# One burst of P·V per group, and new orders of the attention work on three engines

## The chip, the core and the metric

The kernel runs on one core of a Trainium2 chip. The core has five engines that matter here: TensorE (PE, matrix multiplications, its weight loads shown apart as PEld), VectorE (DVE), ScalarE (ACT), GpSimd (POOL), and SyncE (SP), which issues nearly all transfers. Each engine works through its own list of instructions in order and waits on semaphores for the others. The metric is the time of one execution on the device, in microseconds, as the median of several runs.

## The reference

One transformer layer over 8 sequences of 512 tokens and 256 channels, in fp32, with 16 heads of 16 channels:

```python
q, k, v = x @ Wq + bq, x @ Wk + bk, x @ Wv + bv            # per head
probs = softmax(q @ k.T * 16 ** -0.5 + causal)
x = layernorm(x + (probs @ v) @ Wo + bo)
gate = silu((x @ fp8(gate_w)) * gate_scale)
up = (x @ fp8(up_w)) * up_scale
x = layernorm(x + ((gate * up) @ fp8(down_w)) * down_scale)
```

Here `fp8` rounds a weight to float8 and back. The attention and the feed-forward part each have their own residual sum and normalization.

## The kernel before

**Stages.** The program first prepares constants and the projections of the first two sequences (about 30 us), then runs the attention of all sequences, then the feed-forward part of all sequences, whose matrix products keep PE full to the end. The change lies in the attention stage and in the last steps that lead to the feed-forward part.

**Groups.** The attention stage has 32 groups w = 4n + g: n is the sequence (8 of them), g the group of four heads (0 to 3). The text calls a group by w, or by its g where all sequences behave alike. A group on PE holds:

- ten score units, `scores(w, u)`, u = 0 to 9: transposed scores (keys on the partitions) of one or two heads into one of two banks of PSUM, bank u % 2. Units 0 to 3 are the first key block of each head (all 512 queries); units 4 to 7 the second (384 columns) and fourth block (128); units 8 and 9 the third block of two heads each. ACT turns each unit into probabilities (`exps`, L461). A score unit may start only when the exp two units before it is done.
- six units of maxima for the group after the next, `scores_max(w + 2, u)`: scores the other way round, from which DVE reduces each row's maximum (`take_max`, L633). They alternate between two pairs of banks, so that unit u may start only when the reduction of unit u - 2 is done. `split_max` writes the maxima as two bf16 parts, `transpose_max` (L903) turns them into rows, ACT copies them out (`empty_mT`, L447), SP stores them to DRAM and loads them back into the first two rows of the query operand `q_st` (`store_mrow`, `load_mrow`). So the scores of group w + 1 come with the maximum already subtracted.
- the product of the probabilities with V, `attend(w, j)` for the key blocks j = 0 to 3, in four column strips of 32, one for each of the four heads, with a column of ones that gives the sum. Before the change it comes in two bursts: `attend_first(w)` (block 0, L997) near the end of group w, and `attend_rest(w)` (blocks 1 to 3) after unit 3 of group w + 1. ACT empties the result (`empty_y`, L466), PE transposes it (`transpose_y`, L919), DVE divides by the sums (`normalize_y`, L647 and L650), and PE transposes pairs of groups into `ynT` (`transpose_yn`, L930).
- four quarters of `work(n, g, i, half)`, i and half being 0 or 1: for g = 0 and 2 the projections q and k of the next sequence (`project_qk`, L878), for g = 1 the output projection of the last sequence (`project_o`, L947), for g = 3 the projection v of the next (`project_v`, L886). They share one bank, MB, so that the third quarter may start only when DVE or ACT and DVE have emptied the first half (`take_bank`).

**Parts of q and k.** ACT, DVE and POOL split each q and k into three bf16 parts: `hi_part` (ACT, L437), `rest_part` (DVE, L586), `mid_part` (ACT, L441), `lo_part` (POOL, L380). SP stores the parts (`store_parts`) and loads them back in the layout of the operands (`load_stack`: L248, L249, and the zero rows, L251). The first unit of maxima of group w + 2, which runs in group w, is the first reader of stack w + 2.

**Order of SP.** SP's list for one sequence is fixed: stack 3; store and load the maxima of group 1; store the parts 0 and 1 of the next sequence; maxima of group 2; stacks 0 and 1 of the next sequence; maxima of group 3; parts 2 and 3; the next x transposed; maxima of group 0 of the next sequence; its stack 2; its residual x; and, in the first three sequences, one raw feed-forward weight (`load_raw`).

**Other work of the attention stage.** DVE rounds the raw weights in 96 steps (`quantize`, L600 to L614, three steps per group from w = 5 on, the rest in w = 30 and 31), and sums up the residual (`empty_o`), its statistics (`take_stats`) and moments (`take_moments`, L676 to L680). POOL zeroes the masked triangle of the probabilities (`mask_units`, L385) and adds the output bias (`add_bias`, L376) in g = 3. In the last sequence the normalized x of the first two sequences is transposed (`first_hT`, L1015, `h_hi` on ACT, `h_lo` on DVE, L693).

## Time and profile before

| | us |
|---|---|
| median of 3 runs (554.30 to 556.21) | 554.45 |
| profiled execution, its own time | 557.38 |
| its span, first to last instruction | 555.7 |
| PE busy in the span | 527.9 (95%) |
| DVE busy | 459.4 (83%) |
| ACT busy | 316.1 (57%) |
| POOL busy | 227.3 (41%) |
| mean granted clock of PE, of full speed | 0.986 |

Times in the rows below are microseconds from the start of the span. The starts of successive rows of a timeline give what a piece really took from the engine; the duration of a matmul in the trace includes its way through the array, so that successive ones overlap. In brackets stands the idle time before the row and what ended it. The profiled execution lies 2.9 us above the median of the runs.

### The profile page before, as it was taken

To read this page: it belongs to the slowest core of one execution; us is meant where nothing else is said; L and a number is where in the kernel's file an instruction comes from. 1 tells how busy PE (TensorE), PEld (TensorE's weight loads), DVE (VectorE), ACT (ScalarE), POOL (GpSimd) and SP (SyncE) were. 2 spreads that over 40 slices of the span, in tenths; PEclk is the share of its full clock that TensorE was granted. 3 is DMA by queue.
4 is the path that set the end of the run, shared out by engine and by line. 5 is a ranking of instruction groups with operands and counts; after the bars stand their busy time and mean duration, and the time that the engine had idled before them with its cause. 6 is when DMAs were issued, how large, how long until landed. Compare 5 with 4: busy or idle time off the path is not lost.

```text
span 555.7 us, 10699 instructions
## 1 busy us (share of the span) xinstructions
PE 527.9 (95%) x3915; PEld 355.3 (64%) x3917; DVE 459.4 (83%) x808; ACT 316.1 (57%) x579; POOL 227.3 (41%) x251
## 2 busy tenths in 40 slices
PE   8979989999999999999999999998799999999992
PEld 3644546566565655666566565563478888888892
DVE  7876768898898888889888888998748888988876
ACT  3136676667676676766766657667354454436540
POOL 5003343263254334335325434423334654456542
PEclk9988999999999999999999999999899999999998
DMA  5864876657648547456554754700000101111012
GB/s 182 268 149 145 205 231 199 142 186 220 171 156 211 178 144 203 132 164 184 161 148 158 206 155 136 156 4 2 1 0 1 40 0 39 39 38 35 5 38 76
DMA packets 61548, 68.19 MB, mean 123 GB/s; under 512 B 6328, under 2 KB 55864, under 8 KB 61496
## 3 DMA queue, kind: packets, MB, share of 16 engines
q1 hardware_dynamic: 60664, 66.59, 41.9%
q10 hardware_dynamic: 832, 0.92, 0.5%
q8 instruction: 31, 0.51, 0.4%
q14 instruction: 21, 0.17, 0.1%
HBM read 37.62 MB, written 29.61 MB: 121 GB/s over the span
## 4 chain that ended last, share of the span: by engine, by line
PE 78%; DMA 7%; DVE 6%; issue 4%; SPq 2%; ACT 2%; POOL 1%; POOLq 0%; DVEq 0%; ACTq 0%
PE ps L1036 16%; PE ps L989 11%; PE ps L997 10%; PE ps L878 9%; PE ps L1156 7%; PE ps L970 6%; PE ps L947 5%; PE ps L971 4%; PE ps L886 4%; DMA m_scratch<-mrow 2%; PE ps L919 2%; DMA k_scratch<-part 2%; DMA q_st<-zero_rows 2%; PE ps L930 1%; DVE nmax L633 1%
## 5 line engine op out<-in xcount | busy, mean ns | idle before, releaser
L633 DVE TENSOR_REDUCE nmax<-ps 128x2 f32<-128x1024 f32 (+1 forms) x192 | 196.6, 1040 | 49.9 <-PE ps L971 49.3
L461 ACT ACTIVATE probs<-ps 128x512 f32<-128x512 f32 x320 | 184.1, 597 | 76.8 <-PE ps L989 75.3
L385 POOL TENSOR_SCALAR_AFFINE_SELECT probs<-probs 128x512 f32<-128x512 f32 x128 | 87.1, 694 | 209.1 <-ACT probs L461 209.1
L989 PE MATMUL ps<-q_st,k_st 98*128 98x384 bf16 (+3 forms) x512 | 122.7, 303 | 4.4 <-ACT probs L461 3.7
L412 POOL TENSOR_TENSOR f_l<-f_full,f_h 128x512 fp32r<-128x512 f32 x48 | 63.7, 1328 | 72.2 <-ACT f_h L544 72.1
L970 PE MATMUL ps<-k_st,q_st 98*128 98x256 bf16 (+2 forms) x384 | 82.3, 275 | 5.7 <-DMA k_st<-k_scratch 3.2
L971 PE MATMUL ps<-k_st,q_st 124*128 124x128 bf16 x512 | 84.3, 221 | 0.0
L997 PE MATMUL ps<-probs,v_st 128*32 128x512 f32 (+3 forms) x1024 | 82.5, 438 | 0.0
L989 PEld LDWEIGHTS ps<-q_st,k_st 98*128 98x128 bf16 x512 | 44.2, 99 | 48.9 <-issue 26.8
L539 ACT ACTIVATE sgate<-ps,s_gate 128x512 f32<-128x512 f32 x48 | 32.8, 686 | 60.5 <-PE ps L1036 60.5
L971 PEld LDWEIGHTS ps<-k_st,q_st 124*128 124x128 bf16 x512 | 46.0, 98 | 18.2 <-DVE nmax L633 13.7
L970 PEld LDWEIGHTS ps<-k_st,q_st 98*128 98x128 bf16 x384 | 37.6, 98 | 26.6 <-issue 7.8
L778 DVE SCALAR_TENSOR_TENSOR f_full<-ps,s_up,sgate 128x512 f32<-128x512 f32 x48 | 35.5, 744 | 19.5 <-ACT sgate L539 19.5
L1156 PE MATMUL ps<-w_down,f_h 128*128 128x256 f32 x192 | 45.9, 281 | 0.2 <-POOL f_l L412 0.2
L1156 PE MATMUL ps<-w_down,f_l 128*128 128x256 f32 x192 | 45.8, 281 | 0.0
L380 POOL TENSOR_TENSOR part<-rest,part 128x512 bf16<-128x512 f32 x28 | 32.4, 1158 | 32.6 <-ACT part L441 32.6
L997 PEld LDWEIGHTS ps<-probs,v_st 128*32 128x32 f32 x1024 | 28.6, 109 | 20.6 <-issue 12.7
L1036 PE MATMUL ps<-hT_h,w_gate 128*128 128x512 f32 x96 | 39.7, 414 | 0.0
L1036 PE MATMUL ps<-hT_l,w_gate 128*128 128x512 f32 x96 | 38.3, 399 | 0.0
L1036 PE MATMUL ps<-hT_h,w_up 128*128 128x512 f32 x96 | 38.2, 398 | 0.0
L1036 PE MATMUL ps<-hT_l,w_up 128*128 128x512 f32 x96 | 38.0, 395 | 0.0
L1156 PEld LDWEIGHTS ps<-w_down,f_h 128*128 128x128 f32 x192 | 36.2, 189 | 0.7 <-POOL f_l L412 0.4
(96 smaller groups left out, 823.8 us busy)
## 6 DMA issues: line engine op xcount, KB each, us to landing
q_st<-q_scratch SPq DMA_DIRECT2D x31, 384.0 KB
k_st<-k_scratch SPq DMA_DIRECT2D x31, 384.0 KB
q_scratch<-part SPq DMA_DIRECT2D x16, 384.0 KB, 2.6
k_scratch<-part SPq DMA_DIRECT2D x16, 384.0 KB, 2.8
xT<-in_attn_xT SPq DMA_DIRECT2D x8, 512.0 KB, 3.7
q_scratch<-part SPq DMA_DIRECT2D x16, 256.0 KB, 2.9
resid<-in_attn_x SPq DMA_DIRECT2D x8, 512.0 KB, 5.9
k_scratch<-part SPq DMA_DIRECT2D x15, 256.0 KB, 2.1
```

The lines of the kernel that those rows point to most:

```text
L385: pool.affine_select(out=blocks, in_=blocks, compare_op=ALU.is_ge, fill=0.0, base=0, pattern=[*pattern, [1, P]], channel_multiplier=-1).th ...
L412: pool.tensor_tensor(f_l[:, par, ic, :], f_full[:, ic % 3, :], f_h[:, par, ic, :].bitcast(F32), ALU.subtract).then_inc(flo_ready, 1)
L461: act.activation(probs[:, u, :], ps[:, u % 2, :], ACT.Exp, scale=SCALE).then_inc(exp_done, 1)
L633: dve.tensor_reduce(nmax[:, i, heads[0]:heads[-1] + 1], src, AX.X, ALU.max, negate=True).then_inc(max_taken, 1)
L778: dve.scalar_tensor_tensor(f_full[:, ic % 3, :], ps[:, UP[ic % 3], :], s_up[:, ic:ic + 1], sgate[:, ic % 3, :], ALU.mult, ALU.mult).then_i ...
L878: m = pe.matmul(ps[:, bank, :], wt[:, c, P * t:P * t + P], xT[:, n % 2, c, :], start=c == 0, stop=c == KC - 1)
L970: pe.matmul(ps[:, bank, c0:c0 + P * i], q_st[0:RP, g, h, q], k_st[0:RP, g, h, 0:P * i], start=True, stop=True)
L971: m = pe.matmul(ps[:, bank, c0 + P * i:c0 + P * i + P], q_st[0:RA, g, h, q], k_st[0:RA, g, h, q], start=True, stop=True)
L989: m = pe.matmul(ps[:, u % 2, c0:c0 + T - P * j], k_st[0:RP, g, h, P * j:P * j + P], q_st[0:RP, g, h, P * j:T], start=True, stop=True)
L997: m = pe.matmul(ps[HW * h:HW * h + HW, YB, P * j:T], v_st[:, (w // G) % 2, j, HG * g + h, :], probs[:, u, c0:c0 + T - P * j], start=j == 0 ...
L1036: m = pe.matmul(ps[:, bank, :], wt[:, c, P * ic:P * ic + P], hT[:, par, c, :], start=c == 0 and hT is hT_h, stop=c == KC - 1 and hT is hT_l)
L1156: m = pe.matmul(o, f[:, par, ic, P * tb:P * tb + P], w_down[:, ic, :], start=ic == 0 and f is f_h, stop=ic == IC - 1 and f is f_l)
```

## The change

- P·V: `attend_first` and `attend_rest` become `attend_all(w - 1)`, one burst after unit 3 of group w. The probabilities of the units 0 to 3 get a second buffer (`probs_a`, chosen by w % 2), so that the next group's exps can start before the burst; the other six units stay single (`probs_b`). `pv_done` counts once per group.
- `w_raw` has two buffers instead of three. The third raw weight is loaded into the first one, in sequence 4 instead of sequence 2, after the first weight's rounding.
- PE: the unit 0 of the maxima moves ahead of the score unit 2; unit 1 stays behind the burst but ahead of score unit 4; unit 2 comes before the score unit 6, with `transpose_y`; unit 3 before 7, unit 4 after 8, unit 5 after 9, and `transpose_yn` after it. The third quarter of `work` moves from before score unit 6 to after it; the fourth stays between 7 and 8.
- DVE: `take_stats` and `take_moments` move ahead, to before the reduction of unit 1, `normalize_y` moves behind the reduction of unit 3, and one `h_lo` moves back.
- ACT: the first `hi_part` of a group moves from after exp 2 to after exp 3 and `empty_mT`; one `h_hi` moves ahead by one exp.

The core of the diff (the renaming of `probs` in the places where it is only read by its unit is left out):

```diff
-        w_raw = [sb(f"w_raw{m}", [P, KC * I]) for m in range(3)]
+        w_raw = [sb(f"w_raw{m}", [P, KC * I]) for m in range(2)]
-        probs = carve(NU * T).rearrange("p (u t) -> p u t", u=NU)
+        probs_a = carve(2 * HG * T).rearrange("p (z u t) -> p z u t", z=2, u=HG)
+        probs_b = carve((NU - HG) * T).rearrange("p (u t) -> p u t", u=NU - HG)
+        def prob_unit(w, u):
+            return probs_a[:, w % 2, u] if u < HG else probs_b[:, u - HG]
...
@@ SP
+                if m == 2:
+                    sp.wait_ge(quant, 8 * NQ // 3)
-                sp.dma_start(w_raw[m][:].rearrange("p (k n) -> p k n", k=q),
+                sp.dma_start(w_raw[m % 2][:].rearrange("p (k n) -> p k n", k=q),
-                if n < 3:
-                    load_raw(n)
+                if n in (0, 1, 4):
+                    load_raw(min(n, 2))
@@ ACT
                 if u == 0:
-                    wait(act, pv_done, 2 * (w - 1) + 1)
+                    wait(act, pv_done, w - 1)
                 if u == HG:
-                    wait(act, pv_done, 2 * (w - 1) + 2)
+                    wait(act, pv_done, w)
                     exps(w, 2)
-                    if split:
-                        hi_part(n + 1, g)
...
                     if w + 1 < W:
                         empty_mT(w + 1)
+                    if split:
+                        hi_part(n + 1, g)
                     if w:
                         empty_y(w - 1)
                     exps(w, 4)
+                    if last_n and g > 1:
+                        h_hi(g - 2, g - 2, 1, MB)
                     if split:
                         mid_part(n + 1, g)
                     exps(w, 5)
-                    if last_n and g > 1:
-                        h_hi(g - 2, g - 2, 1, MB)
@@ DVE
                         rest_part(n + 1, g)
+                    if g > 1 and n:
+                        take_stats(n - 1, 2 * g - 4)
+                        take_stats(n - 1, 2 * g - 3)
...
                         h_lo(g - 2, g - 2, 0, MB)
-                    if g > 1 and n:
-                        take_stats(n - 1, 2 * g - 4)
-                        take_stats(n - 1, 2 * g - 3)
+                    if g == 3 and n:
+                        take_moments(n - 1)
                     if more:
                         take_max(w + 2, 1)
                         take_max(w + 2, 2)
-                    if last_n and g > 1:
-                        h_lo(g - 2, g - 2, 1, MB)
-                    if w:
-                        normalize_y(w - 1)
                     if w > G:
                         quantize(first_step(w) + 1)
                     if more:
                         take_max(w + 2, 3)
-                    if g == 3 and n:
-                        take_moments(n - 1)
+                    if w:
+                        normalize_y(w - 1)
                     if split:
                         rest_part(n + 1, g + 1)
+                    if last_n and g > 1:
+                        h_lo(g - 2, g - 2, 1, MB)
@@ PE
-            def attend_first(w):
-                pe.wait_ge(masked, 4 * w + 1)
+            def attend_all(w):
+                pe.wait_ge(masked, 4 * w + 4)
                 wait(pe, yn_ready, w)
                 pe.wait_ge(v_out, 2 * (w // G) + 2)
-                attend(w, 0).then_inc(pv_done, 1)
-            def attend_rest(w):
-                pe.wait_ge(masked, 4 * w + 4)
-                attend(w, 1)
-                attend(w, 2)
-                attend(w, 3).then_inc(pv_done, 1)
+                for j in range(TB - 1):
+                    attend(w, j)
+                attend(w, TB - 1).then_inc(pv_done, 1)
...
-                    scores(w, 2)
                     if more:
                         scores_max(w + 2, 0)
+                    scores(w, 2)
                     scores(w, 3)
                     if w + 1 < W:
                         transpose_max(w + 1)
                     if w:
-                        attend_rest(w - 1)
-                    scores(w, 4)
+                        attend_all(w - 1)
                     if more:
                         scores_max(w + 2, 1)
+                    scores(w, 4)
                     scores(w, 5)
-                    work(n, g, 1, 0)
-                    scores(w, 6)
                     if more:
                         scores_max(w + 2, 2)
                     if w:
                         transpose_y(w - 1)
+                    scores(w, 6)
+                    work(n, g, 1, 0)
+                    if more:
+                        scores_max(w + 2, 3)
                     scores(w, 7)
+                    work(n, g, 1, 1)
+                    scores(w, 8)
                     if w + 1 == W:
...
                         gate_up(0, 0, 0)
-                    work(n, g, 1, 1)
-                    scores(w, 8)
                     if more:
-                        scores_max(w + 2, 3)
+                        scores_max(w + 2, 4)
                     scores(w, 9)
                     if more:
-                        scores_max(w + 2, 4)
-                    attend_first(w)
+                        scores_max(w + 2, 5)
+                    if w + 1 == W:
+                        gate_up(0, 0, 1)
                     if g == 0 and n:
                         transpose_yn(n - 1, 1, w)
                     if g == 3:
                         transpose_yn(n, 0, w if n + 1 < B else None)
-                    if w + 1 == W:
-                        gate_up(0, 0, 1)
-                    if more:
-                        scores_max(w + 2, 5)
-            attend_rest(W - 1)
+            attend_all(W - 1)
```

## Rows read from the trace of the kernel before

**Rows 1.** Busy time by stretch: us, busy of PE, PEld, DVE, ACT, POOL, clock, DMA.

```profile
240.31:251.50 11.19, 11.19 (x92) 6.05 (x90) 10.07 (x18) 8.06 (x16) 3.97 (x5) 1.00 0.46 138
251.50:263.18 11.68, 11.68 (x104) 8.04 (x102) 10.49 (x24) 6.91 (x14) 7.00 (x8) 1.00 0.65 189
263.18:274.76 11.58, 11.58 (x96) 6.51 (x94) 9.89 (x18) 8.32 (x17) 4.53 (x6) 1.00 0.64 178
274.76:285.96 11.20, 11.20 (x100) 7.55 (x98) 9.74 (x16) 7.34 (x14) 3.77 (x5) 1.00 0.53 153
```

**Rows 2.** Timeline of PE around the two bursts of P·V (both lie between rows).

```profile
238.93 0.22 PE L971 MATMUL ps<-k_st,q_st 124*128 124x128 bf16 x1
...
240.08 0.40 PE L971 MATMUL ps<-k_st,q_st 124*128 124x128 bf16 x4
...
240.53 1.02 PE L878 MATMUL ps<-xT,w_q 128*128 128x512 f32 x2
241.39 0.38 PE L989 MATMUL ps<-q_st,k_st 98*128 98x512 bf16 x1
...
243.13 0.38 PE L989 MATMUL ps<-q_st,k_st 98*128 98x512 bf16 x1
...
244.90 0.39 PE L989 MATMUL ps<-q_st,k_st 98*128 98x384 bf16 x2
```

**Rows 3.** Timeline of PE: third quarter of work in g = 2, then in g = 0.

```profile
245.47 0.38 PE L989 MATMUL ps<-q_st,k_st 98*128 98x384 bf16 x2
...
246.70 0.38 PE L989 MATMUL ps<-q_st,k_st 98*128 98x384 bf16 x2
...
268.34 0.38 PE L989 MATMUL ps<-q_st,k_st 98*128 98x384 bf16 x2
...
269.47 0.39 PE L989 MATMUL ps<-q_st,k_st 98*128 98x384 bf16 x2
```

**Rows 4.** Timelines of PE and ACT: last quarter's hi_part, and a wait for an exp.

```profile
248.03 1.07 PE L878 MATMUL ps<-xT,w_k 128*128 128x512 f32 x2
...
249.20 0.69 ACT L437 ACTIVATE part<-ps,b_k 128x512 bf16<-128x512 f32 x1 [0.38 <-PE ps L878]
...
69.70 1.68 ACT L461 ACTIVATE probs<-ps 128x512 f32<-128x512 f32 x3
...
70.35 0.39 PE L989 MATMUL ps<-q_st,k_st 98*128 98x512 bf16 x1 [0.47 <-ACT probs L461]
```

**Rows 5.** Timelines of ACT, SP, PE and PEld: maxima out, a stack's last issue, its reader.

```profile
255.25 0.25 ACT L447 ACTIVATE mrow<-ps 32x128 bf16<-32x128 bf16 x1
...
242.69 0.32 PE L970 MATMUL ps<-k_st,q_st 98*128 98x384 bf16 x1
...
146.12 0.65 SPq L251 DMA_DIRECT2D q_st<-zero_rows  x1
...
150.91 0.10 PEld L970 LDWEIGHTS ps<-k_st,q_st 98*128 98x128 bf16 x1 [0.57 <-DMA q_st<-zero_rows]
```

**Rows 6.** Chain of waits, 100 to 345 us: total us, times, longest.

```profile
PEld ps L970 <- DMA q_st<-zero_rows: 1.9, 4, 0.7
```

**Rows 7.** Timelines of DVE and POOL: g = 3, and the bias of the last sequence.

```profile
254.53 1.23 DVE L633 TENSOR_REDUCE nmax<-ps 128x2 f32<-128x1024 f32 x1 [0.61 <-PE ps L971]
...
257.45 0.93 DVE L633 TENSOR_REDUCE nmax<-ps 128x2 f32<-128x768 f32 x1
...
261.92 0.37 DVE L676 BATCH_NORM_AGGREGATE moments<-stats 128x2 f32<-128x6 f32 x4
...
256.02 2.46 POOL L376 TENSOR_TENSOR resid<-resid,b_o 128x1024 f32<-128x1024 f32 x1
...
388.30 2.44 POOL L376 TENSOR_TENSOR resid<-resid,b_o 128x1024 f32<-128x1024 f32 x1
...
388.57 2.38 DVE L610 TENSOR_SCALAR q_d<-q_d 128x384 f32<-128x384 f32 x1
```

**Rows 8.** Timeline of PE in the last group.

```profile
392.20 0.66 PE L1015 MATMUL ps<-ident,resid 128*128 128x128 f32 x4 [3.70 <-DVE hT_l L693]
```

More of the change, by code:

```diff
@@ L210, in attention_over @@
         def attention_over(eng):
-            for s, count in [(st_full, NU * W), (max_full, NM * W), (pv_done, 2 * W), (mT_full, W),
+            for s, count in [(st_full, NU * W), (max_full, NM * W), (pv_done, W), (mT_full, W),
                              (late_in, 16 * NLATE), (scales_in, 16 * NSCALE)]:
@@ L764, in _ @@
                         take_max(w + 2, 4)
+                    if more:
                         take_max(w + 2, 5)
+                    if more:
                         split_max(w + 2)
```

33 lines of the change are left out of this document (17 added, 16 removed).

## The prediction

> **What bounds the kernel now.** I read the busy time by stretch first, then the timeline of PE over four groups, then those of DVE, ACT and SP beside it. In the attention's steady state a sequence is four groups of 11.19, 11.68, 11.58 and 11.20 us (g = 2, 3, 0, 1), together 45.65, and PE is busy in all of it, at full clock, DVE in 9.7 to 10.5 of each [rows 1]. So PE's stream sets the pace there, and only what shortens it or makes it wait counts. From w = 5 to w = 27 this pattern runs 23 groups. Before it (w = 0 to 4) PE waits for stacks and maxima from DRAM, after it (w = 28 to 31) for DVE. The feed-forward part is untouched.
>
> Inside the stream there are costs that no idle time shows. An fp32 matmul of 512 columns takes 0.86 us (240.53 to 241.39), a bf16 one of 128 columns 0.06 and one of 512 0.22 [rows 2].
>
> **One burst instead of two.** The first burst lies between the matmuls that start at 238.93 and 240.08: 1.15, less 0.06 of the first one, is 1.09 us for what streams in 0.86. The other, with `transpose_max` in front, lies between 243.13 and 244.90: 1.77 less 0.22 is 1.55, for 384 + 256 + 128 = 768 columns, 1.28 at that rate [rows 2]. Each burst so costs about 0.25 beyond its columns. One burst has 0.86 + 1.28 + 0.27 = 2.41 instead of 2.64: 0.23 less per group, 23 x 0.23 = 5.3 us. If the surplus belonged to the key blocks and not to the burst, it would be nothing.
>
> The Trainium skill says that a change of tiling mode drains TensorE (TensorEngine Tiling (Array Packing), Key Properties). It names no price; that the surplus stands at both bursts agrees with it.
>
> **The third quarter of work.** In g = 2 it takes, with the score unit before it, 245.47 to 246.70 = 1.23 us; in g = 0, where its bank has long been free, 268.34 to 269.47 = 1.13 [rows 3]. The 0.10 is the wait for DVE, which empties the bank just then; g = 1 and 3 have it too. The change puts the quarter 1.9 us later in the group (burst of block 0, maxima unit 2, `transpose_y` and score unit 6 now precede it), and DVE does nothing later there: 17 groups x 0.09 = 1.5 us gained. `transpose_yn` no longer follows a burst directly, which gives about 0.05 in 11 groups, 0.5.
>
> **The end of a group.** After the fourth quarter PE now has only score unit 8 (0.22), maxima unit 4 (8 matmuls of 128 columns, 0.46), score unit 9 (0.22) and maxima unit 5 (4 of them, 0.23) before the next group, together 1.13. ACT's order there is as before: `hi_part`, exp 8, exp 9. `hi_part` starts 1.17 after the start of the fourth quarter (248.03 to 249.20) and takes up to 0.69, an exp frees its bank 0.65 after its start (69.70 to 70.35) [rows 4]. So unit 0 of the next group can start 1.17 + 0.6 + 0.65 = 2.42 after the quarter's start, where PE would be there after 0.91 (the 0.86 and the entry after a short matmul) + 1.13 = 2.04. In g = 0 and 3 `transpose_yn` covers it (0.49 before, the difference of g = 3 to g = 2 in [rows 1]). In g = 2 it doesn't: 0.38 us in 6 groups, 2.3 lost. Before, maxima unit 3 and the burst lay there as well and covered it.
>
> **The moments.** In g = 3 `take_moments` moves ahead to before the reduction of unit 1. DVE comes to it about here: the reduction of unit 0 started 3.03 us into the group (254.53 less 251.50), now 0.22 earlier, 2.81, and from it to the end of the statistics it takes 257.45 - 254.53 = 2.92; so at 5.7, and with the 0.37 of the four aggregations the copy of the means comes at about 6.1. `add_bias` started 4.5 into the group (256.02) and follows exp 3, which comes about 0.25 later (below): 4.8, and 2.46 long, to 7.2 [rows 1, 7]. The one case in the trace of a DVE instruction of the tensor_scalar or copy kind under that addition is at 388.57: it took 2.38 us, to 390.95, the addition ran 388.30 to 390.74 [rows 7]. If the copy of the means is held likewise, to 7.3, the reduction of unit 1 starts 1.1 later, and that of unit 3 ends at 10.6, just where PE wants it for unit 5; `normalize_y` and `empty_v` then end at 11.9, and the first quarter of the next group wants the bank at 11.6. That costs 0.3 to 0.5 a sequence; 6 x 0.4 = 2.4 lost. Below: nothing, if so small a copy slips through; above: 1.1 x 6 = 6.6, if nothing is absorbed. I take 2.4, since the row shows the hold but the reductions have slack.
>
> The Trainium skill says that VectorE's modes with two ports and its instructions with two SBUF inputs contend with GpSimd for the SBUF interface (GPSIMD Engine Reference, Specifications). The row at 388.57 agrees; by the rule alone the copy waits, so the term stays.
>
> **Transfers.** Four weight loads between 100 and 345 us waited for a stack's last transfer, 1.9 us in total, 0.7 the longest [rows 6]. They read the stacks 8, 12, 14 and 18, which so had no slack. For stack 12 the last issue is at 146.12, the reader at 150.91, 4.79 later [rows 5]. The chain to a stack goes over the maxima in the same queue of SP: `empty_mT`, store, load, stack. The reader comes now 2.16 into its group instead of 2.38 (240.31 to 242.69), as the maxima precede the score unit 2, and the group before it is shorter by 0.33 to 0.37. And `empty_mT`, 3.75 into g = 3 before (251.50 to 255.25) [rows 1, 5], stands behind exps 2 and 3, and score unit 2 starts 0.44 later than before, so that the two exps ((1.68 - 0.60) / 2 = 0.54 apart [rows 4]) follow at 3.0 and 3.5 and `empty_mT` at about 4.0. Together each stack is wanted about 0.8 earlier against its issue. For the stacks without slack that is up to 0.8 of waiting each, less the 0.4 of the moments in g = 3 for stacks 14 and 18. The third of the four (stack 14) has the third raw weight behind it; with that weight's load the delay moves to stack 22. I take 4 places x 0.5 = 2.0 lost, less 0.3 that the first pass loses at the old place: 1.7. Ends: 0 (the stores land when the traffic ahead of them is through, however late they are issued), and 4.7 (all six stacks after g = 1 and g = 3 that lie within 1 us).
>
> **Start and end.** In w = 0 there is no burst any more (-1.1), but `hi_part` comes after exp 3, behind a stack that lands late, and the exp wait above applies in w = 0 and 2; where a stack is waited for, score unit 2 now lies behind it (+0.22) and the maxima's copy comes later (+0.3), twice. Together +0.4, between -1 and +1.5. At the end PE waits 3.70 us for `h_lo` on DVE [rows 8]; statistics of two blocks (0.66) now stand before that `h_lo`, and the last burst, 0.86 longer, follows the last work: of both I count 1.2, as one score unit, `transpose_y` and one burst's surplus leave that stretch. Between 0 and 2.5.
>
> **Sum.** -5.3 - 1.5 - 0.5 + 2.3 + 2.4 + 1.7 + 0.4 + 1.2 = +0.7 us. Against the profiled execution, 557.38 us, that is 558.1; the median of the runs is 554.45, so 555.1. POOL's own orders are unchanged, its mask of units 8 and 9 ends some 1.3 us into the next group by the exps' times above and is wanted after score unit 3, at 3.1; the second buffer of `probs_a` takes away a wait for the burst that nothing else now has. SP's new wait for `quant` in sequence 4 is met by then (32 steps are done in w = 15).
>
> **Rivals.**
>
> 1. *The hidden costs don't come* (faster). The moments' copy isn't held and the stacks land in time: -4.1 more, so 551.0; if the exp wait is covered too, 548.7. For it: DVE's 128 x 4 copy is tiny, and the store of the maxima is only 8 KB behind bigger transfers. Against: rows 6 and 7. It decides from a stack delay under 0.2 us and a hold under 0.3.
> 2. *The stacks become the bound* (slower). The time from `empty_mT` to the stack's last byte doesn't shrink with the group. If it grows by 0.5 (the parts of g + 1 are now stored later and lie before the maxima's store), the wait applies to 13 stacks at about 0.5, another +5: 560. For it: the four waits already there. Against: from w = 18 on no weight load shows one. It decides from 0.8 us later than now.
> 3. *The burst's surplus stays* (slower). It belongs to the blocks: +5.3, 560.4. Against: the second burst has three blocks and about the surplus of the one.
> 4. *DVE becomes the bound in g = 0 and 2*: `rest_part` comes after the last quarter, so `split_max` ends 14.1 into the group, where PE wants it at 14.3. If late by 0.3 in 12 groups: +2.2 after what the exp wait absorbs, 557.3.
>
> **Chances.** Forecast 0.40 (with its own range 552.0 to 557.2); rival 1 0.33; rival 2 0.13; rival 3 0.05; rival 4 0.09, of which half reads as no change. Likeliest is 555.1. The range reaches from rival 1 to rival 2: 549.5 to 560. About 0.5%, 2.8 us, is what a measurement of this kernel can tell from no change. Faster 0.34, same 0.42, slower 0.24.
>
> **What would show it.** P·V: x1024 as before, but one burst per group, 2.4 us between its neighbours. `issue` and ACT: weight loads of unit 0 wait for exp 8 by 0.3 to 0.4 in g = 3. DVE: L680 in g = 3 takes over 1 us. PEld waits for the zero rows more than 4 times, over 2 us. The third quarter's 0.10 is gone in g = 1, 2, 3. The period of four groups is 44.8 to 45.3 instead of 45.65. The prediction is wrong if the period comes below 44.7 (rival 1) or if g = 2 and 0 become longer than 11.6 without `transpose_yn` (rivals 2 and 4).

## The result, and the profile after

The kernel after takes 562.98 us (560.56 to 563.85, four runs) against 554.56 of before beside it: 1.0138 times, 95% interval 1.0102 to 1.0175. Ratios here and below are worked out from the single runs and not from the two medians, and leave out runs over 1.5% above the fastest of their kernel (three of `mom_late`, one of `moments_back`, one of before). The kernel after is slower by 1.4%; 555.1 was predicted, and the range ended at 560. The profiled execution took 562.99 us, its span 561.3, 5.6 more than before. Counted by the starts of the groups' first score units, 0.95 us of the 5.6 arise before w = 5, 2.3 in the 23 groups from w = 5 to 27, where a gain of 0.9 was expected, and 2.4 after.

Busy time by stretch of the kernel after, of w = 17 to 20 (g = 1, 2, 3, 0; the last three are the first three groups of [rows 1]):

```profile
231.25:242.32 11.07, 11.07 (x99) 7.64 (x98) 9.73 (x17) 7.08 (x15) 3.79 (x5) 1.00 0.49 146
242.32:253.63 11.31, 11.02 (x93) 6.17 (x90) 9.91 (x17) 8.03 (x16) 3.83 (x5) 1.00 0.50 143
253.63:265.11 11.48, 11.48 (x102) 8.01 (x102) 10.93 (x24) 7.14 (x14) 5.96 (x6) 1.00 0.64 185
265.11:277.66 12.55, 11.74 (x95) 6.39 (x93) 10.33 (x16) 8.20 (x17) 4.75 (x6) 1.00 0.72 186
```

Against [rows 1], g = 1 is shorter by 0.13 and g = 3 by 0.20; g = 2 is longer by 0.12 and g = 0 by 0.97. The four take 46.4 together instead of 45.65, where 44.8 to 45.3 was forecast. The last column but two is the granted clock: it is full in both.

Timeline of PE, in w = 21 (a burst), in w = 22 (the end of g = 2) and in w = 16:

```profile
280.97 1.08 PE L1008 MATMUL ps<-probs_a,v_st 128*32 128x512 f32 x8
281.86 1.49 PE L1008 MATMUL ps<-probs_b,v_st 128*32 128x384 f32 x24
283.28 0.28 PE L981 MATMUL ps<-k_st,q_st 98*128 98x256 bf16 x1
...
299.14 0.38 PE L1000 MATMUL ps<-q_st,k_st 98*128 98x256 bf16 x2
299.36 0.39 PE L982 MATMUL ps<-k_st,q_st 124*128 124x128 bf16 x4
300.04 0.38 PE L1000 MATMUL ps<-q_st,k_st 98*128 98x512 bf16 x1 [0.29 <-ACT probs_b L469]
...
222.09 0.34 PE L981 MATMUL ps<-k_st,q_st 98*128 98x384 bf16 x1 [1.10 <-DMA q_st<-zero_rows]
```

The whole burst takes 283.28 - 280.97 = 2.31. Before, the second burst took 1.45 and the first 1.00, with 0.10 lost in front of it ([rows 2]: 1.15 less 0.06); 2.55 has become 2.31, so the saving of 0.24 per group is real. But four maxima matmuls that stream in 0.23 (299.36) are followed by a score unit only 0.68 later: 0.45 of waiting for exp 8, at the end of each g = 2. And in w = 16 the first maxima unit waits for a stack.

The chain of waits from 100 to 345 us:

```profile
PEld ps L981 <- DMA q_st<-zero_rows: 6.8, 6, 1.9
PE ps L981 <- DMA q_st<-zero_rows: 2.2, 3, 1.1
PE ps L1000 <- ACT probs_b L469: 1.7, 6, 0.3
```

The stacks' row is 6.8 us in six waits, where it was 1.9 in four [rows 6]. All the long ones stand in g = 0, for the stack of g = 2. Timeline of SP before the row at 222.09:

```profile
208.80 0.33 SPq L244 DMA_DIRECT2D k_scratch<-part  x1
209.24 0.38 SPq L270 DMA_DIRECT2D xT<-in_attn_xT  x1
211.05 0.33 SPq L260 DMA_DIRECT2D m_scratch<-mrow  x1
214.25 0.64 SPq L264 DMA_DIRECT2D q_st<-m_scratch  x1
215.00 0.34 SPq L253 DMA_DIRECT2D q_st<-q_scratch  x1
```

The 8 KB of maxima are stored at 211.05, and SP waits 3.2 us for them, until 214.25, before it loads them and then the stack. 512 KB of x transposed were issued 1.8 us ahead of them. That neighbour isn't new. In the kernel before, the same group has:

```profile
207.85 0.38 SPq L265 DMA_DIRECT2D xT<-in_attn_xT  x1
209.66 0.33 SPq L255 DMA_DIRECT2D m_scratch<-mrow  x1
212.19 0.64 SPq L259 DMA_DIRECT2D q_st<-m_scratch  x1
```

There too the load is issued 1.8 us ahead, and the store takes 2.5 us. Last, the moments, on DVE and POOL in g = 3:

```profile
306.35 1.21 DVE L687 TENSOR_SCALAR veps<-moments 128x4 f32<-128x4 f32 x1
307.47 0.16 DVE L688 COPY means<-moments 128x4 f32<-128x4 f32 x1
307.54 2.07 DVE L641 TENSOR_REDUCE nmax<-ps 128x2 f32<-128x768 f32 x2
```

POOL's bias addition ran from 305.17 to 307.53, and `veps` ended with it.

### The profile page after: what moved, and what is told of

The parts are those of the page before. It is cut to its first block, busy times and chain, and to the rows that moved or that the text cites. A ratio compares the mean times of both kernels' runs of the same rounds, so it can differ in the third digit from the quotient of the medians.

```text
span 561.3 us, 10698 instructions
## 1 busy us (share of the span) xinstructions
PE 525.5 (94%) x3915; PEld 356.8 (64%) x3917; DVE 462.9 (82%) x808; ACT 314.4 (56%) x579; POOL 222.1 (40%) x251
## 4 chain that ended last, share of the span: by engine, by line
PE 67%; DMA 10%; DVE 8%; ACT 4%; issue 4%; SPq 3%; POOL 1%; POOLq 0%; DVEq 0%; ACTq 0%
PE ps L1043 15%; PE ps L1008 10%; PE ps L1000 8%; PE ps L1161 7%; PE ps L889 7%; PE ps L981 6%; DMA q_st<-zero_rows 6%; PE ps L958 5%; DVE nmax L641 3%; PE ps L982 3%; PE ps L897 2%; DMA m_scratch<-mrow 2%; PE ps L930 2%; DMA k_scratch<-part 2%; PE ps L1022 1%
## 5 line engine op out<-in xcount | busy, mean ns | idle before, releaser
L641 DVE TENSOR_REDUCE nmax<-ps 128x2 f32<-128x1024 f32 (+1 forms) x192 | 194.2, 1040 | 36.9 <-PE ps L982 35.4
L469 ACT ACTIVATE probs_b<-ps 128x512 f32<-128x512 f32 x192 | 109.0, 596 | 37.5 <-PE ps L1000 35.5
L1000 PE MATMUL ps<-q_st,k_st 98*128 98x384 bf16 (+3 forms) x512 | 113.6, 303 | 6.9 <-ACT probs_b L469 5.3
L393 POOL TENSOR_SCALAR_AFFINE_SELECT probs_b<-probs_b 128x512 f32<-128x512 f32 x96 | 61.1, 654 | 105.1 <-ACT probs_b L469 105.1
L469 ACT ACTIVATE probs_a<-ps 128x512 f32<-128x512 f32 x128 | 71.8, 597 | 50.7 <-PE ps L1000 50.6
L981 PEld LDWEIGHTS ps<-k_st,q_st 98*128 98x128 bf16 x384 | 37.7, 98 | 44.8 <-issue 18.8
L393 POOL TENSOR_SCALAR_AFFINE_SELECT probs_a<-probs_a 128x512 f32<-128x512 f32 x32 | 22.2, 694 | 110.4 <-ACT probs_a L469 110.4
L1008 PEld LDWEIGHTS ps<-probs_b,v_st 128*32 128x32 f32 x768 | 28.4, 114 | 37.0 <-issue 32.7
L1008 PE MATMUL ps<-probs_b,v_st 128*32 128x384 f32 (+2 forms) x768 | 50.2, 394 | 0.0
L474 ACT ACTIVATE yT<-ps 128x512 f32<-128x512 f32 x32 | 19.1, 597 | 40.5 <-PE ps L1008 40.5
```

Source lines behind the costliest of these rows:

```text
L393: pool.affine_select(out=blocks, in_=blocks, compare_op=ALU.is_ge, fill=0.0, base=0, pattern=[*pattern, [1, P]], channel_multiplier=-1).th ...
L469: act.activation(prob_unit(w, u), ps[:, u % 2, :], ACT.Exp, scale=SCALE).then_inc(exp_done, 1)
L641: dve.tensor_reduce(nmax[:, i, heads[0]:heads[-1] + 1], src, AX.X, ALU.max, negate=True).then_inc(max_taken, 1)
L981: pe.matmul(ps[:, bank, c0:c0 + P * i], q_st[0:RP, g, h, q], k_st[0:RP, g, h, 0:P * i], start=True, stop=True)
L1000: m = pe.matmul(ps[:, u % 2, c0:c0 + T - P * j], k_st[0:RP, g, h, P * j:P * j + P], q_st[0:RP, g, h, P * j:T], start=True, stop=True)
L1008: m = pe.matmul(ps[HW * h:HW * h + HW, YB, P * j:T], v_st[:, (w // G) % 2, j, HG * g + h, :], prob_unit(w, u)[:, c0:c0 + T - P * j], start ...
```

## The experiments

Ratios are to the kernel before in the same series, with their 95% intervals; before had medians of 556.2 to 557.0 us in these series. A "piece" is the time from the start of one unit's matmuls to the start of the next.

### First series: one part alone, or one part back

`burst_alone` is the kernel after with the lists of PE, DVE and ACT in the order of before: one burst after score unit 3 and nothing else moved. `pe_order_back` has only PE's list in the old order. `moments_back` has only this undone on DVE:

```diff
-                    if g == 3 and n:
-                        take_moments(n - 1)
                     if more:
                         take_max(w + 2, 1)
...
                     if more:
                         take_max(w + 2, 3)
+                    if g == 3 and n:
+                        take_moments(n - 1)
```

`raw_alone` is the kernel before with two raw buffers and the third load in sequence 4.

> The changed kernel with the orders of PE, DVE and ACT put back to those of before: what is left of the change is the single burst, the second buffer of the units 0 to 3 and the raw weight's later load. Theory A (the burst gains, the new orders lose): about 0.23 us per group in 23 steady groups, 1.1 more in w = 0, so 548 to 550 us, ratio to before 0.988 to 0.992; the steady period of four groups is 44.7 to 44.9 instead of 45.65. Rival B (the burst itself loses, because the stacks become the bound at any shorter period): ratio at or over 1.0, with waits for the zero rows over 1 us in g = 0.

> The changed kernel with PE's order of units put back to that of before (one burst, after score unit 3); DVE and ACT keep the new orders. Theory A (PE's new order causes the stack waits, by a later score unit 9, a later empty_mT and an earlier reader): the waits for the zero rows fall back to 0.7 us or less each, ratio to before 0.99 to 1.00. Rival (the orders of DVE and ACT cause them, by the parts stored later): ratio stays over 1.01.

> The changed kernel with take_moments alone put back behind the reduction of unit 3 in g = 3. The changed kernel's veps instruction takes 1.2 us there under POOL's addition of the bias. If that hold costs what the prediction said, 0.3 to 0.5 us a sequence: about 2.4 us faster than the changed kernel, 560.5, ratio to before 1.010. Rival (the hold is absorbed, since PE waits for the stack in the next group anyway): the same time as the changed kernel within 0.5 us, ratio 1.014.

> The kernel before with two raw weight buffers and the third weight's load moved from sequence 2 to sequence 4, nothing else. Theory A: within 0.1% of before (0.3 us gained at stack 14 and in w = 12, as much lost at stack 22). Rival: the load in sequence 4 makes stack 22 late by over 1 us, ratio 1.002 to 1.004.

| | us | ratio |
|---|---|---|
| burst_alone | 571.91 | 1.0261 (1.0232 to 1.0290) |
| pe_order_back | 584.31 | 1.0491 (1.0457 to 1.0524) |
| moments_back | 563.04 | 1.0081 (1.0051 to 1.0111) |
| raw_alone | 555.99 | 0.9978 (0.9957 to 0.9998) |

The raw weights are not the cause: `raw_alone` is 0.2% faster than before, if anything. The single burst in the old orders loses 2.6%, nearly twice as much as the whole change. So the theory that the burst gains and the new orders lose fell: the new orders repair about half of what the burst breaks. They do so only together. `pe_order_back` keeps the new orders of DVE and ACT under the old one of PE, and loses 4.9%, where no loss was expected. In its profile no weight load waits for the zero rows from 100 to 345 us, as expected, but PE now waits for DVE instead: 3.3 us in five waits for `rest_part` (`rest`), 5.4 in five for `normalize_y` (`yn`), and 3.0 in five for the residual sum (`resid`). Windows of `burst_alone`, g = 2, 3, 0, then the end of g = 2 on PE:

```profile
243.17:254.80 11.63, 11.26 (x92) 6.14 (x90) 10.16 (x18) 7.82 (x15) 3.69 (x6) 1.00 0.48 138
254.80:267.15 12.35, 11.80 (x105) 8.15 (x102) 10.74 (x24) 7.00 (x14) 7.16 (x8) 1.00 0.65 183
267.15:279.56 12.41, 11.77 (x96) 6.61 (x94) 9.88 (x17) 8.31 (x17) 4.93 (x6) 1.00 0.81 223
```

```profile
253.98 0.22 PE L979 MATMUL ps<-k_st,q_st 124*128 124x128 bf16 x1
254.57 0.40 PE L979 MATMUL ps<-k_st,q_st 124*128 124x128 bf16 x4 [0.37 <-DVE nmax L641]
254.80 0.38 PE L997 MATMUL ps<-q_st,k_st 98*128 98x512 bf16 x1
255.22 0.92 PE L894 MATMUL ps<-w_v,xT 128*128 128x256 f32 x3
```

Where the first burst used to stand, between maxima units 4 and 5, PE now waits 0.5 us (254.57 less 253.98 less 0.06) for the reduction of unit 3. The next group's first quarter comes another 0.2 late (255.22 less 254.80 less 0.22) and takes 0.1 longer. That is more than the 0.24 saved. This gave the new theory: the first burst was cover for DVE and ACT at the end of a group.

The hold of the moments was left undecided: the time fell by some 0.6% against the 1.0138 of another series, but in the profiles the 23 groups take 265.1 against 265.5 us, since stacks that land late take back most of it.

### Second series: what is PE's work worth?

`cut_before` and `cut_after` leave out 384 of the 512 queries of key block 0 of P·V:

```diff
-                    m = pe.matmul(ps[HW * h:HW * h + HW, YB, P * j:T], v_st[...],
-                                  probs[:, u, c0:c0 + T - P * j], start=j == 0, stop=j == TB - 1)
+                    m = pe.matmul(ps[HW * h:HW * h + HW, YB, P * j:T if j else P], v_st[...],
+                                  probs[:, u, c0:c0 + (T - P * j if j else P)], start=j < 2, stop=j == TB - 1 or j == 0)
```

`pad_burst` adds to `burst_alone`, between maxima units 4 and 5, the four matmuls of block 0 once more, for nothing. `two_bursts` is the kernel after with the first burst back between score unit 9 and maxima unit 5.

> The kernel before with key block 0 of P.V multiplied for its first 128 queries alone (it leaves out the other 384 columns of that block in every group), so that the first burst of a group, near its end, streams 128 columns instead of 512: 0.65 us less of PE's work per group, with nothing moved. Theory P (the prediction's: PE's stream sets the pace in the steady state, so what shortens it counts in full): 0.65 x 31 = 20 us less, 537. Theory C (the first burst covers work of DVE and ACT at a group's end: reductions whose banks the next maxima and the transposition want, exps 8 and 9; without it PE waits there): at most a third of it comes, 549 to 555, and the chain of waits shows PE waiting for the reductions of nmax.

> The kernel after with the same cut (the single burst streams 1280 - 384 = 896 columns; it leaves out 384 columns of block 0). Theory P: 20 us less than after, 543. Theory C with the stacks: the burst lies in the middle of the group, where DVE and ACT have slack, but the stacks from DRAM and exp 8 bound g = 0 and 2, so the groups shrink by the cut in g = 1 and 3 alone: 8 to 14 us less, 549 to 555, with more waiting for the zero rows.

> The single burst with all orders of before (571.9), and with a pad at the place of the old first burst: the same four matmuls of block 0 into the bank of y, whose result the real burst overwrites. It is PE work for nothing, 1.1 us in each of 32 groups. Theory P: 35 us more, 607. Theory C: the pad lies in waits that are there already (the weight loads of the transposition and of the next scores waited for nmax): 572 to 580, and these waits vanish from the chain.

> The kernel after, but with P.V in two bursts again: block 0 between score unit 9 and maxima unit 5 of its own group, blocks 1 to 3 at the place of the single burst; the double first key blocks, the raw weights and all other orders are those of after. Theory P: the surplus of 0.23 us comes back in about 27 groups: 6 us more than after, 569. Theory C: the first burst covers again exp 8 in g = 2 and 1, and the end of the reductions: these waits go (0.3 in 12 groups), the stack is wanted later by as much as the burst lies behind its issue; 559 to 563, same as after or below. If it falls under 556, the single burst itself is what costs, also on the new orders.

| | us | ratio |
|---|---|---|
| cut_before | 552.29 | 0.9915 (0.9888 to 0.9942) |
| cut_after | 547.78 | 0.9855 (0.9806 to 0.9903) |
| pad_burst | 577.84 | 1.0387 (1.0347 to 1.0427) |
| two_bursts | 564.13 | 1.0137 (1.0104 to 1.0170) |

In `cut_before` the first burst's piece falls from 1.00 to 0.44 us. Its windows, g = 1, 2, 3, 0:

```profile
226.71:237.35 10.64, 10.63 (x101) 7.55 (x98) 9.30 (x15) 7.33 (x14) 3.64 (x6) 1.00 0.50 153
237.35:248.23 10.88, 10.87 (x93) 6.02 (x90) 10.07 (x18) 7.90 (x15) 3.68 (x6) 1.00 0.52 148
248.23:259.80 11.57, 11.37 (x105) 8.02 (x102) 10.63 (x24) 7.01 (x14) 7.14 (x8) 1.00 0.60 180
259.80:271.35 11.55, 11.27 (x96) 6.48 (x94) 9.88 (x17) 8.30 (x17) 4.93 (x6) 1.00 0.74 190
```

Against [rows 1] that is 0.56 less in g = 1, 0.31 in g = 2, 0.11 in g = 3 and next to nothing in g = 0. In all 31 groups 17 us of PE's work went and the time fell by 4.7 (0.85% of 556; the interval is 3.2 to 6.2). In the kernel after, the same cut (0.64 a group in the single burst, 20 us) brings 2.8%, 15.7 us, more than was expected by the theory of cover and less than by that of PE's pace. Its place is another, the middle of the group, but so is the kernel, and the 1.0138 comes from another series. `pad_burst` is the mirror: 32 x 1.1 = 35 us of useless work on `burst_alone` cost 1.26%, 7 us. So PE was busy throughout in the kernel before, but other engines were almost as late as PE at the end of the group.

`two_bursts` has after's time. In its g = 3 (12.97 us) PE waits 0.75 for the reduction of maxima unit 1, which stands behind the held moments, and 0.64 for the first burst, whose bank `normalize_y` empties late in the new DVE list. It doesn't tell the burst's worth.

### Third series: after's waits, one by one

`xt_after` moves one load of SP, `xt_before` does the same to before:

```diff
                 load_mrow(n, 3)
+                if n + 2 < B:
+                    load_xT(n + 2)
                 if nxt:
                     store_parts(n + 1, 2)
                     store_parts(n + 1, 3)
-                if n + 2 < B:
-                    load_xT(n + 2)
```

`hi_after` puts the second `hi_part` behind exp 8. `mended` has this, the early load, `moments_back`, and the third quantize step ahead of `rest_part`.

> The kernel after, where SP issues the load of the next x transposed (512 KB) behind the load of the maxima of group 3, ahead of the stores of the parts 2 and 3, instead of behind them and so ahead of the maxima of the next group 0. Theory S (in after, the stores of these maxima wait behind the 512 KB, and with them the stack of g = 2, whose landing PE waits for in g = 0 and in the start): the store takes 2.4 us instead of 3.2 to 3.7, stacks 4, 6, 18, 22, 26 and 30 land about 1 us earlier, the zero rows' 9.0 us of waits fall under 3, g = 0 takes 11.7 every time; 4 us less than after, 558 to 560. Rival: the stack is limited by its own 768 KB and the load of x that goes with it; then nothing changes, 562 to 564.

> The kernel after, where the second hi_part of a group comes behind exp 8 on ScalarE, not ahead of it. Theory E (the next group's first score unit waits for exp 8, which stands behind hi_part, 0.45 us in g = 2 and about 0.2 with the entry of the matmul behind it): g = 2 takes 10.8 instead of 11.30, g = 3 0.1 less, 3 to 4 us less than after over 6 passes if the stacks don't take it back, 559. If the stacks set the pace of a pass, all of it is given back in g = 0: 562 to 563, with g = 2 short and g = 0 longer than 12.4.

> The kernel after with four things mended at once: x transposed loaded earlier (as in the run before the last), hi_part behind exp 8, the moments behind the reduction of maxima unit 3, and VectorE's third quantize step of a group ahead of rest_part (which waits for hi_part there, 9.5 us in all), no longer behind it. PE's stream without waits would be 10.9, 10.8, 11.2 and 11.3 us in g = 1, 2, 3 and 0, 44.2 against 45.65 of before. Theory C with S and E: the waits were all that stood against the burst's gain; the pass takes 44.3 to 45.0, 551 to 555. If the first half of the old burst is needed as cover whatever is mended, the pass stays at 46 and the time at 560.

> The kernel before with x transposed loaded earlier alone, as a control. Before waits 1.9 us for the zero rows of four stacks in the steady state, and more in its start: theory S expects 1 to 3 us less than before, 553; the rival, no change.

| | us | ratio |
|---|---|---|
| xt_after | 559.02 | 1.0039 (1.0016 to 1.0061) |
| hi_after | 568.63 | 1.0208 (1.0172 to 1.0244) |
| mended | 570.00 | 1.0233 (1.0201 to 1.0265) |
| xt_before | 554.35 | 0.9953 (0.9934 to 0.9971) |

The stacks' theory held: 1.0138 has become 1.0039. Timeline of SP in `xt_after`, in the same group as above:

```profile
209.59 0.33 SPq L260 DMA_DIRECT2D m_scratch<-mrow  x1
210.97 0.64 SPq L264 DMA_DIRECT2D q_st<-m_scratch  x1
```

The maxima's store takes 1.4 us instead of 3.2, and the waits for zero rows fall from 6.8 us in six to 2.4 in five. The store isn't short every time: in w = 23 it takes 3.1 us even so (3.7 in after), and in w = 28 PE waits 3.1 us for a stack (1.9 in after). The load also helps the kernel before.

`hi_after` removed its wait and lost more, beyond both times that were expected. The end of its g = 2:

```profile
257.79 0.39 PE L982 MATMUL ps<-k_st,q_st 124*128 124x128 bf16 x4
258.04 0.38 PE L1000 MATMUL ps<-q_st,k_st 98*128 98x512 bf16 x1
259.38 0.92 PE L897 MATMUL ps<-w_v,xT 128*128 128x256 f32 x3 [0.97 <-DVE rest L594]
```

Score unit 0 no longer waits (0.25 after unit 5 of the maxima), but the first quarter starts 1.34 after it instead of 0.22, since `rest_part`, behind the later `hi_part`, empties its bank. The fourth quarter, `hi_part`, `rest_part` and exps 8 and 9 are one chain; whoever goes first, PE has too little behind the fourth quarter to cover it. `mended` has the same wait (1.34 in w = 19) and missed both of its expected times; its further parts can't be read apart.

### Fourth and fifth series: cover, moments, and the burst again

`ty_late` is `xt_after` with `transpose_y` behind the fourth quarter in g = 2, and the third quantize step ahead of `normalize_y` there:

```diff
+                    late = n + 1 < B and g == 2
-                    if w:
+                    if w and not late:
                         transpose_y(w - 1)
                     scores(w, 6)
...
                     work(n, g, 1, 1)
+                    if late:
+                        transpose_y(w - 1)
                     scores(w, 8)
```

`mom_late` is `xt_after` with `take_moments` behind `empty_v(n + 1, 1)`. `both_late` has both, and in the last sequence maxima unit 0 behind score units 2 and 3. `xt_raw_before` is before with the early load and the two raw buffers. `both_two_bursts` is `both_late` with the first burst back between score unit 9 and maxima unit 5. `ends_back` is `both_late` with maxima unit 0 behind units 2 and 3 in the first sequence too, and the last sequence's `h_lo` at their old places on DVE.

> The kernel after with x transposed loaded earlier (xt_after, 559.0 us), and in g = 2 the transposition of y behind the fourth quarter of work instead of ahead of score unit 6, with VectorE's third quantize step ahead of normalize_y there. That puts 0.44 us of PE between the fourth quarter and the end of the group, without holding anything else of the group's end. Theory E (the fourth quarter, hi_part, exp 8 and rest_part are a chain that needs about 0.45 us more cover than after's order leaves in g = 2): g = 2 takes 10.85 instead of 11.30, g = 3 0.17 less at its start; 3 to 4 us less than xt_after, 555.5. Rival: the chain moves to the bank of the next group's first quarter, as when hi_part was put behind exp 8; 559 or more.

> xt_after, and take_moments behind the emptying of the second half of v, where POOL's bias addition has ended. Theory M (VectorE, held about 1.0 us by that addition, has no idle time in g = 3 and comes late to the second half of v, whose bank the next group's first quarter wants: 0.32 us of waiting and 0.1 of entry at the start of g = 0, 0.07 in the third quarter): g = 3 and g = 0 lose these 0.5 together, 5 passes, 2.5 us less than xt_after, 556.5. Rival: the hold is absorbed; 559.

> Both of these, and in the last sequence maxima unit 0 behind the score units 2 and 3 (its stack lands 3 us late there and nothing lies behind it). If E and M hold and add up: 559.0 - 3.5 - 2.5 - 0.5 = 552.5, better than before (556.9 in that series) and than before with the earlier load (554.4). Rival: the shorter groups wait for the stacks; 556.

> The kernel before with the two changes that helped it alone: x transposed loaded earlier, and two raw weights with the third loaded in sequence 4. Both act on the stacks' landings, so they add up only where they mend other ones: 552.5 to 554.5.

> The kernel both_late (554.2) with P.V in two bursts again, the first between score unit 9 and maxima unit 5, all else as it is. It asks what the single burst is worth once the waits at its side are mended. In both_late's steady groups PE waits only about 0.4 at the start of g = 3 and 0.06 in g = 2. Theory P: the surplus of 0.24 us comes back in about 25 groups, 6 us more, 560. Theory C, that the first burst's place covers what it costs: in g = 2 and g = 3 its 1.0 us lies in no wait any more, but normalize_y, which it waits for, comes late in DVE's list: 558 to 566. If it is under 555, the single burst is worth nothing even here.

> The kernel both_late with the two ends nearer to before: in the first sequence too, maxima unit 0 behind score units 2 and 3; in the last, VectorE's two h_lo ahead of the statistics and of the quantize step, as before. both_late's start (w = 5 at 91.8 us) and its last four groups (32.0 us) are 6 and 2.3 us longer than those of before with the earlier load; its steady passes are 0.5 us shorter each. If these orders are what the ends lose by: start 1 to 2 us and tail 1 us less, 552. If the ends are set by the stacks that land late and by exps, no change: 554.

| | us | ratio |
|---|---|---|
| ty_late | 559.13 | 1.0061 (1.0035 to 1.0086) |
| mom_late | 556.22 | 0.9979 (0.9948 to 1.0010) |
| both_late | 554.19 | 0.9966 (0.9947 to 0.9985) |
| xt_raw_before | 555.02 | 0.9969 (0.9945 to 0.9994) |
| both_two_bursts | 559.24 | 1.0044 (1.0018 to 1.0071) |
| ends_back | 554.97 | 0.9961 (0.9933 to 0.9989) |

`ty_late` shortened g = 2 from 11.30 to 11.08, but the next group's first quarter waits 0.3 instead of 0.06 for `rest_part`, and the time didn't change: a miss. `mom_late` came out as expected: `veps` takes 0.17 us (the row of its line in g = 3), g = 3 has lost its small waits, and g = 0 takes 11.3 to 11.5 where no stack is late (the windows of g = 3 and 0) instead of 11.7, since the first quarter finds its bank empty:

```profile
L687 DVE TENSOR_SCALAR veps<-moments x1: 171/171/171, 261.6 to 261.6; 128x4 f32<-128x4 f32 x1
```

```profile
250.06:261.54 11.48, 11.48 (x101) 8.10 (x102) 10.31 (x22) 7.13 (x14) 5.95 (x6) 1.00 0.68 197
261.54:273.03 11.49, 11.48 (x95) 6.47 (x93) 9.80 (x17) 8.20 (x17) 4.86 (x6) 1.00 0.73 199
```

`xt_raw_before` isn't faster than `xt_before`, so its two changes don't add up. `both_late` is faster than before by 0.34% and than after by 1.7%, but not faster than `xt_before` (0.9953), the kernel before with the one line moved: no complete kernel here with the single burst is. Its windows (g = 2, 3, 0, 1), and those of `both_two_bursts`, g = 2, 3:

```profile
239.32:250.40 11.08, 11.05 (x93) 6.16 (x90) 10.11 (x18) 7.95 (x16) 3.94 (x5) 1.00 0.51 137
250.40:262.14 11.74, 11.57 (x104) 8.09 (x102) 10.30 (x21) 7.39 (x14) 5.97 (x6) 1.00 0.68 202
262.14:273.45 11.31, 11.31 (x95) 6.56 (x93) 9.80 (x17) 8.20 (x17) 4.86 (x6) 1.00 0.74 192
273.45:284.52 11.07, 11.07 (x99) 7.64 (x98) 9.73 (x18) 7.07 (x15) 3.78 (x5) 1.00 0.63 201
```

```profile
241.06:253.14 12.08, 11.44 (x93) 5.90 (x91) 10.06 (x18) 8.62 (x16) 4.00 (x6) 1.00 0.63 175
253.14:264.69 11.55, 11.55 (x104) 7.89 (x102) 10.00 (x24) 6.49 (x12) 6.25 (x7) 1.00 0.55 156
```

Four groups take 45.20 against 45.65 in [rows 1]. With two bursts the time rises by 0.8%, 4.3 us, but that is an upper end for the single burst's worth, not the worth itself. In g = 0, without waits in either, 11.54 (w = 24) stands against 11.31, the 0.23 of the surplus. In g = 2 there is 1.0 more, and 0.68 of it is the first burst's wait for `normalize_y`, which stands late in an order of DVE that was made for one burst. In g = 3 two bursts are shorter by 0.19, as they cover `rest_part`. Two bursts with an order of DVE of their own were not tried on this kernel.

`ends_back` isn't told apart from `both_late`. Its profiled execution reaches w = 5 at 87.1 us instead of 91.8 but spends 33.7 in w = 28 to 30 instead of 31.9. Before with the early load needs 86.2 and 29.7 there. So the ends take back what the middle gains against `xt_before`. At the start the granted clock tells the cases apart. The kernel before itself reached w = 5 at 91.5 us, with two raw buffers at 86.9. Granted clock in 40 slices of the span, of before, of after, and of `raw_alone`:

```profile
PEclk9988999999999999999999999999899999999998
PEclk9979999999999999999999999999899999999997
PEclk9999999999999999999999999999799999999996
```

In before's profile the clock is 0.50, the lower of its two levels (1.2 instead of 2.4 GHz), from 38.1 to 45.0 us, after PE stood idle from 34.8 to 38.0. The profiles of `raw_alone`, `xt_before`, `xt_raw_before` and `ends_back` have the full clock up to 100 us, and all four reach w = 5 between 85.6 and 87.1; those of before, after, `xt_after` and `both_late` have 6.8 to 10.2 us at the lower level there, and reach it between 91.4 and 92.4. So a start can't be read from one profile without its clock. What `ends_back` loses in w = 28 to 30 was not settled.

## Why the prediction was wrong

The measured time lies 7.9 us above 555.1. Of that 3.2 arise in w = 5 to 27, 0.55 before, 1.2 after, and 2.9 come from the step from the profile to the median. By the starts of PE's pieces, the terms of the middle came out so (us):

| term | forecast | measured |
|---|---|---|
| one burst | -5.3 | -5.3 |
| third quarter of work | -1.5 | -1.9 |
| `transpose_yn` | -0.5 | -0.5 |
| end of a group | +2.3 | +4.5 |
| moments | +2.4 | +2.1 |
| transfers | +1.7 | +3.4 |
| sum | -0.9 | +2.3 |

- **The steps that failed** are two terms of the sum, the end of a group (4.5 instead of 2.3) and the transfers (3.4 instead of 1.7). Both are waits that the single burst and the new orders lay open.
- **One burst instead of two** was right as a cost: 0.24 a group against 0.23. What did not hold as it stands is "So PE's stream sets the pace there, and only what shortens it or makes it wait counts". PE was indeed never idle, but DVE was almost as late as PE: of what is taken from PE at the first burst's place, only about a quarter comes back (`cut_before`: 4.7 of 17 us). The first burst was priced as a burden and hardly as cover, though the prediction did see its cover for exp 8 in g = 2. Gone alone, with all else in place, it leaves waits of 0.5 + 0.2 + 0.1.
- **The end of a group** was right in kind, but too small and too narrow. The wait for exp 8 in g = 2 is 0.45 instead of 0.38. The next group's first quarter adds 0.16 in g = 3, and 0.17 in five of the six g = 1: 6 x 0.61 + 5 x 0.17 = 4.5 us against 2.3. What was taken for one late exp is a chain that `rest_part` belongs to, as `hi_after` and `ty_late` showed.
- **Transfers** had the right kind of wait and half its size. Late stacks hold PE 3.0 us from w = 5 to 27 (0.26, 1.27, 0.83 and 0.65 in w = 6, 16, 20 and 24), a late load of maxima 0.37; in w = 28 PE waits 1.9 for a stack once more. The prediction counted how much later the issues stand against the reader, and that was right: from the store of the maxima to the reader of the stack of g = 2 there are 9.6 to 9.8 us where no stack is late, 10.0 to 10.2 before, 0.4 less. It left out that the store itself takes a different time in every pass: in w = 7 to 23 of g = 3, 1.8 to 2.5 us before and 2.0 to 3.7 after, with x transposed issued 1.8 to 1.9 us ahead of it in both kernels. Why it takes longer after in w = 15 and 23 is open. That the big load is part of it is shown: the one line that `xt_after` moves brings 1.0% (1.0138 to 1.0039, from two series), and 3.1 us in w = 5 to 27 of the profiles. Rival 2, the stacks, came nearest with 560, but it expected 13 late stacks, and it is those of g = 2 that hold PE.
- **The moments** were right in kind and size: held as in [rows 7], 1.21 us. The one held is `veps`, though, and not the copy of the means (0.16), which the prediction named. The first quarter in g = 0 takes 0.42 longer in five groups, 2.1 against 2.4. From `xt_after` to `mom_late` it is 0.6%, 3.3 us, or 0.4% with the three runs that the ratio leaves out.
- **The third quarter of work** lost its 0.10 in g = 2 and 0.08 in g = 1, as said. In g = 3 it lost 0.08 in one half of the groups and 0.20 in the other, where it had waited longer before; the rest is the emptying of v behind the held moments.
- **Start and end**: 0.95 and 2.4 us against 0.4 and 1.2. The clock has part in both. The windows below end with the granted clock, in the last column but two: start and end of the attention stage in the kernel before, then both in the kernel after.

```profile
31.20:91.50 60.30, 53.65 (x428) 29.12 (x426) 42.21 (x59) 38.31 (x72) 20.51 (x26) 0.94 0.67 182
354.70:414.00 59.30, 51.87 (x399) 32.64 (x397) 45.85 (x89) 35.93 (x66) 19.19 (x23) 0.97 0.09 22
18.15:92.41 74.26, 63.24 (x496) 36.13 (x497) 50.98 (x70) 37.85 (x72) 19.87 (x25) 0.93 0.68 192
357.92:402.00 44.08, 37.19 (x306) 20.92 (x304) 38.23 (x77) 27.09 (x53) 13.27 (x17) 0.92 0.17 38
```

At the start the profile of the kernel after has the lower of the two clocks, 0.50, for 10.2 us (before 6.8), at the end of the attention for 6.8 (before 3.4). In between it is full in both. Each of the two differences of 3.4 us can account for up to 1.7 us, an estimate: half of them, as PE does half as much there. The prediction had no term for the clock. The wait for the stack in w = 28 is part of the 2.4 too.
- **From the profile to the median**: 2.9 us of the miss come from carrying down the sum by the distance of one profiled execution to three runs. Before's medians in the later series (556.2 to 557.0) lie nearer to the profile.
- The Trainium skill's rule that a change of tiling mode drains TensorE (TensorEngine Tiling (Array Packing), Key Properties) agrees with the 0.23 in g = 0 between one burst and two. The Trainium skill's rule on the SBUF interface of VectorE and GpSimd (GPSIMD Engine Reference, Specifications) agrees with `veps`: 1.21 us under the addition, 0.17 outside it.

## What to carry to other kernels

An engine that is busy all the time isn't proof that shortening its list shortens the kernel: cut a piece of it (or pad it) at the very place, and see how much comes back, before paying for the cut with anything. Work at the end of a group is cover for the chains that start there, so when it is moved, look for what else can stand there. In this case no order with the single burst came out faster than the old order with one line of SP moved. And look for a small store that a chain waits for behind a big load in the same queue: this one line was worth 0.5% before the change and 1.0% after it.

## What was not expected of the hardware

- A wait of PE cost more than its length here. When a first quarter starts late, the piece after its start is about 0.1 us longer: in the kernel before, 251.72 to 252.59, 0.87 us; in `ty_late`, after a wait for `rest`, 251.81 to 252.78, 0.97 us. In `cut_before`, where 0.56 us of the stream went, g = 2 is only 0.31 shorter: its score unit 0 is followed 0.14 late, and the piece behind takes 0.10 more.

```profile
251.81 1.13 PE L899 MATMUL ps<-w_v,xT 128*128 128x256 f32 x4 [0.16 <-DVE rest L594]
252.78 0.38 PE L1002 MATMUL ps<-q_st,k_st 98*128 98x512 bf16 x1
```

- A TENSOR_SCALAR of VectorE with 4 columns took 1.21 us under GpSimd's two-input addition and 0.17 outside it: the hold lasts to the end of the other instruction, however small the held one is.
- An 8 KB store took 3.2 us from its issue to the next issue of SP with 512 KB issued 1.8 us ahead, and 1.4 without (w = 15). Over the five passes it was 2.0 to 3.7 with the load ahead, and 1.4 in four of five without.
- The spread of the runs goes with the clock. The runs of the kernel before that show a mean granted clock of 0.980 take 558.3 us on average (15 runs), those with 0.988 or more 554.5 (11 runs). In `xt_after` the four runs with 0.981 to 0.984 take 556.0 to 557.3, the six with 0.975 to 0.978 take 559.3 to 562.3. Which comes first, the waits or the lower clock, no run here tells.
